# Heads in every fourth partition, x and the second context behind the first fills, and the last weights loaded later

## The chip, the cores and the metric

The kernel runs on one NeuronCore of a Trainium2 chip. The number that counts is the device time of one execution in microseconds. The kernel before was timed three times. One further execution was recorded by the profiler, and all rows below come from that one.

## What is computed

A cross-attention layer with an MLP behind it, for 8 batches of 256 queries over 1601 keys, width 256, 16 heads of 16.

```python
q = layer_norm(x) @ q_w + q_b ;  k = ctx @ k_w + k_b ;  v = ctx @ v_w + v_b      # per head of 16
attn = softmax(where(mask, q @ k.T / sqrt(16), min));  out = attn @ v
hidden = out @ cproj_w + cproj_b + x
y = gelu(layer_norm(hidden) @ fc_w + fc_b) @ proj_w + proj_b
return hidden + y
```

## The kernel before

Five instruction streams are written out by hand, one for each engine, and semaphores join them. For each batch K is computed with three products of split operands (a high and a low part), V and Q likewise. Four heads make a slot, so a batch has four slots. Each slot has 13 key tiles, hence 52 steps a batch, in 26 pairs. In a step TensorE multiplies the slot's `kst` (keys as weights) with `qst` (queries) into the PSUM tensor `S` (line 1119), ScalarE takes the exponential of all 1024 columns into `pr` (line 583), and TensorE multiplies `pr` with `vsl` into `O` (line 1126). Into the pairs of batch b are woven the projections of batch b+1 (`K_AT`, `V_AT`, pairs `XT_AT`, `Q_AT`) and the sampled maxima of a slot (`max_unit`, line 1106, pairs `MAX_AT`): slots 2 and 3 of the running batch at pairs 3 and 9, slots 0 and 1 of the next at pairs 15 and 21. Batch 0 has no batch ahead of it, so a head part does its projections and the maxima of its slots 0 and 1 first, with TensorE's order `v7, max(0,0), v8, max(0,1), v9, v10, max(1,0), v11, max(1,1), v12`.

K goes by way of HBM. VectorE splits it into `kpart` (lines 725, 728), SP stores it to `k_scr` (`store_k`, line 386), one unit for each of two halves of the width and four chunks of the keys, and `fill` brings it back into `kst`. A head of a slot takes 64 partitions of `kst`, two heads above each other (`g_` = 0, 1) and two side by side (`j`). Before, its first 32 partitions hold the high and low parts of K, 16 more the high part again, then comes the mask row (48) and the row of the maxima (49), and 14 partitions are unused. `qst` is laid out to match. One slot is 192 rows of 1601 floats of K, 96 rows of 512 floats of Q and four mask rows, 1.45 MB in all, in 10 DMAs, five for each half of the partitions. `kst` has places for four slots, which are used in turn.

DMAs are issued on two queues, SP's and ScalarE's (ACT's). Before the fills of batch 0 six small DMAs (`constant_rows`) write the rows of ones and the padding, on SP. On ACT the order of the head is: the high parts of the four context chunks (`high`), the loads of the second batch's context (`next_ctx`, four chunks, 1.64 MB), the second half of slot 0's fill, the fills of slots 1 and 2, and then the exponentials. `first_fill` for slot 2 waits until all eight K units of the batch have landed in HBM. On SP the load of the rest of x (12 row tiles, 1.57 MB, needed by VectorE at pair 6) stands behind the first batch's context. The mlp's weights `fc_raw` and `pj_raw` lie over the tiles of the projections; `load_mlp` on ACT waits for the last K, Q and V of batch 7, then issues two loads, and GpSimd splits the weights (lines 539 to 543). VectorE needs the first of the two low parts at pair 13 of batch 7, ACT both at step 36.

```python
for b in range(B):
    for n in range(STEPS):
        ...
        if n == 44 and b + 2 == B:
            load_mlp()
        ...
        exponential(first, b, n)
```

Of the kernel before, what the change touches and what calls it, by code (L numbers as in the profile page):

```python
# [42 lines left out]
H, HD = 16, 16  # L43
# [3 lines left out]
QT = LQ // P  # L47
# [16 lines left out]
MASKROW, MAXROW = 3 * HD, 3 * HD + 1  # L64
# [109 lines left out]
def build(nc, x, ctx_t, mask, w_kv, w_qc, fc, pj, cols, rows, ident, out):  # L174
    stack = ExitStack()
    with stack:
# [103 lines left out]
        o_zeroed, again_zeroed = sem("o_zeroed"), sem("again_zeroed")  # L280
# [62 lines left out]
        def fill(eng, s_, b, s, halves=range(2)):  # L343

            rows_of = k_scr[bass.ds(b, 1), s // 2].rearrange("o r (d h) t -> (o r d) h t", h=HM)
            for g_ in halves:
                r0, h0 = g_ * HALF, HG * (s % 2) + NJ * g_
                eng.dma_start(kst_d[r0:r0 + 2 * HD, s, :, 0:LK], rows_of[:, h0:h0 + NJ, 0:LK]).then_inc(s_.slot_in[s], 16)
                eng.dma_start(kst_d[r0 + 2 * HD:r0 + 3 * HD, s, :, 0:LK], rows_of[0:HD, h0:h0 + NJ, 0:LK]
                              ).then_inc(s_.slot_in[s], 16)  # L350
                eng.dma_start(kst_d[r0 + MASKROW:r0 + MASKROW + 1, s, :, 0:LK],
                              mask_scr[bass.ds(b, 1), :].unsqueeze(1).broadcast_to([1, NJ, LK])
                              ).then_inc(s_.slot_in[s], 16)
                for r, copies in ((0, 2), (1, 1)):
                    eng.dma_start(qst_d[r0 + 2 * HD * r:r0 + 2 * HD * r + copies * HD, s, :, :].rearrange("p j q -> p (j q)"),
                                  q_scr[bass.ds(b, 1), s // 2, r].rearrange("o (d h) q -> o d (h q)", h=HM)[
                                      :, :, h0 * LQ:(h0 + NJ) * LQ].broadcast_to([copies, HD, NJ * LQ])
                                  ).then_inc(s_.slot_in[s], 16)

        FILLS = 10  # L360
# [9 lines left out]
        def first_fill(eng, b, s, halves=range(2)):  # L370
# [8 lines left out]
            fill(eng, first, b, s, halves)  # L379

        @block.sync
        def _(sp):
# [38 lines left out]
            sp.dma_start(hid[:, 2 * QT:TOK, :], x[2 * QT:TOK].rearrange("n p d -> p n d")).then_inc(xrest_in, 16)  # L421
# [7 lines left out]
            sp.wait_ge(pads_set, 3)  # L429
            constant_rows()  # L430

            for c in range(CH):
                store_k(0, 0, c)
            store_q(0)
            first_fill(sp, 0, 0, [0])
# [3 lines left out]
            first_rows(0, 1)  # L439
# [916 lines left out]
```

## Time and profile before

| what | us |
|---|---|
| three runs | 768.25, 773.13, 775.28 |
| median | 773.13 |
| profiled execution, device time | 768.76 |
| its span, first to last instruction | 767.0 |
| TensorE busy in the span | 702.5 |
| ScalarE busy | 446.1 |
| VectorE busy | 371.3 |
| GpSimd busy | 120.9 |

Busy times are sums over instructions of an engine. The span is 1.8 us shorter than the device time of the same execution. Weight loads of TensorE run beside its products and are a row of their own (PEld).

### The profile page before, as it was taken

The numbers are of one execution on the slowest core, as the hardware profiler recorded it, in microseconds if no ns is written. First come the engines' busy times: TensorE is split into PE (matmuls) and PEld (weight loads), VectorE is DVE, ScalarE is ACT, GpSimd is POOL, SyncE is SP. The second block draws the span as 40 slices with busy tenths as digits, with TensorE's granted clock in tenths as the row PEclk, the third lists the DMA queues.
The fourth block names the chain that finished last, engine by engine and source line by source line (L and its number), as shares of the span: only waits on it lengthen the run. The fifth ranks groups of instructions, "written<-read, shape, count | busy, mean of one in ns | idle before, by whom it ended". The sixth has DMA issues, their size and how long they took to land.

```text
span 767.0 us, 16866 instructions
## 1 busy us (share of the span) xinstructions
PE 702.5 (92%) x7026; PEld 478.5 (62%) x7026; DVE 371.3 (48%) x824; ACT 446.1 (58%) x475; POOL 120.9 (16%) x90
## 2 busy tenths in 40 slices
PE   3657699899999999999999999999998978999997
PEld 3545466566656656666566566656664544597897
DVE  6643355265436534643464446534642331467663
ACT  3004366856676677567756775676566788733321
POOL 5222002200220032003201220131000600110010
PEclk9867799999999999999999999999999989999999
DMA  9787578657874788477938694878475800000000
GB/s 312 216 186 131 186 184 188 179 138 183 189 203 128 174 188 217 143 180 158 235 123 203 148 246 123 192 153 230 132 165 126 253 6 2 1 21 8 29 28 31
DMA packets 51275, 113.78 MB, mean 148 GB/s; under 512 B 7050, under 2 KB 40178, under 8 KB 49914
## 3 DMA queue, kind: packets, MB, share of 16 engines
q1 hardware_dynamic: 40700, 80.47, 44.5%
q10 hardware_dynamic: 10494, 32.17, 13.8%
q8 instruction: 58, 0.95, 0.6%
q14 instruction: 23, 0.19, 0.1%
HBM read 65.30 MB, written 47.06 MB: 146 GB/s over the span
## 4 chain that ended last, share of the span: by engine, by line
PE 76%; ACT 13%; DMA 5%; DVE 3%; issue 2%; ACTq 1%; DVEq 0%
PE O L1126 21%; PE S L1119 16%; ACT pr L583 11%; PE O L1056 10%; PE XB L1056 10%; PE O L1213 6%; PE S L1056 6%; DMA k_scr<-kpart 2%; DMA qst<-q_scr 2%; PE XB L1093 2%; PE XB L1153 2%; PE MB L1106 2%; DVE kpart L725 1%; DVE kpart L728 1%; DMA cols_s<-in_cols 1%
## 5 line engine op out<-in xcount | busy, mean ns | idle before, releaser
L583 ACT ACTIVATE pr<-S 128x1024 f32<-128x1024 f32 x416 | 400.6, 1024 | 188.6 <-PE S L1119 184.4
L1126 PE MATMUL O<-pr,vsl 128*17 128x256 f32 x3328 | 227.4, 388 | 1.3 <-DVE ot L790 1.3
L1119 PEld LDWEIGHTS S<-qst,kst 50*128 50x128 f32 x1664 | 117.1, 188 | 120.4 <-ACT pr L583 81.4
L1119 PE MATMUL S<-qst,kst 50*128 50x256 f32 x1664 | 171.7, 315 | 18.7 <-ACT pr L583 15.0
L1126 PEld LDWEIGHTS O<-pr,vsl 128*17 128x17 f32 x3328 | 75.3, 97 | 79.2 <-issue 17.7
L725 DVE TENSOR_SCALAR kpart<-O,cols_s 128x384 fp32r<-128x384 f32 x64 | 40.6, 635 | 120.7 <-PE O L1056 120.7
L771 DVE TENSOR_REDUCE mx<-MB 128x2 fp32r<-128x512 f32 x64 | 44.1, 690 | 79.0 <-PE MB L1106 79.0
L510 POOL CAST c_hi<-cT 128x768 fp32r<-128x768 f32 (+1 forms) x28 | 23.9, 852 | 348.0 <-DMA cT<-in_ctx_t 235.8
L1056 PE MATMUL XB<-w_hi,c_hi 128*128 128x256 f32 (+1 forms) x208 | 68.3, 328 | 2.1 <-DVE vsl L739 1.3
L739 DVE TENSOR_TENSOR vsl<-XB,rows_s 128x256 f32<-128x256 f32 (+1 forms) x104 | 43.3, 417 | 55.1 <-PE XB L1056 55.1
L1056 PE MATMUL O<-c_hi,w_hi 128*128 128x384 f32 (+1 forms) x128 | 52.6, 411 | 17.7 <-POOL c_lo L515 10.3
L515 POOL TENSOR_TENSOR c_lo<-cT,c_hi 128x768 fp32r<-128x768 f32 (+1 forms) x32 | 60.9, 1904 | 8.9 <-ACT c_hi L571 6.7
L1056 PE MATMUL XB<-w_lo,c_hi 128*128 128x256 f32 (+1 forms) x208 | 60.5, 291 | 0.0
L1056 PE MATMUL XB<-w_hi,c_lo 128*128 128x256 f32 (+1 forms) x208 | 60.1, 289 | 0.0
L601 ACT ACTIVATE g<-S,cols_s 128x512 f32<-128x512 f32 x32 | 22.1, 690 | 57.1 <-PE S L1056 52.8
L790 DVE STREAM_TRANSPOSE ot<-O 128x256 f32<-128x256 f32 x32 | 14.4, 450 | 78.0 <-PE O L1126 77.2
L1056 PEld LDWEIGHTS XB<-w_hi,c_hi 128*128 128x128 f32 (+1 forms) x208 | 40.1, 193 | 17.3 <-issue 9.0
L1056 PE MATMUL O<-c_lo,w_hi 128*128 128x384 f32 (+1 forms) x128 | 45.7, 357 | 0.0
L1056 PE MATMUL O<-c_hi,w_lo 128*128 128x384 f32 (+1 forms) x128 | 45.5, 355 | 0.0
L1106 PE MATMUL MB<-kst,qst 49*128 49x256 f32 x128 | 29.8, 314 | 16.3 <-DMA qst<-q_scr 16.2
L774 DVE TENSOR_REDUCE mx<-O 128x2 fp32r<-128x512 f32 x64 | 43.6, 682 | 0.0
L728 DVE SCALAR_TENSOR_TENSOR kpart<-O,cols_s,kpart 128x384 fp32r<-128x384 f32 x64 | 40.6, 635 | 2.3
(100 smaller groups left out, 825.6 us busy)
## 6 DMA issues: line engine op xcount, KB each, us to landing
kst<-k_scr SPq DMA_DIRECT2D x59, 400.2 KB
k_scr<-kpart SPq DMA_DIRECT2D x48, 384.0 KB, 8.0
v_scr<-vsl ACTq DMA_DIRECT2D x8, 1768.0 KB, 11.9
kst<-k_scr SPq DMA_DIRECT2D x59, 200.1 KB
cT<-in_ctx_t ACTq DMA_DIRECT2D x21, 384.0 KB, 7.6
k_scr<-kpart SPq DMA_DIRECT2D x16, 449.0 KB, 7.1
q_scr<-qpart SPq DMA_DIRECT2D x16, 256.0 KB, 2.5
qst<-q_scr SPq DMA_DIRECT2D x59, 64.0 KB
```

Source lines behind the costliest of these rows:

```text
L515: nc.gpsimd.tensor_tensor(c_lo[:, c, :, 0:n], cT[:, c, :, 0:n], c_hi[:, c, :, 0:n].bitcast(F32), ALU.subtract).then_inc(lo_done, 1)
L583: nc.scalar.activation(pr[:, n % PBUF, :], S[:, 2 * (n % 2):2 * (n % 2) + 2, :] .rearrange("p a n -> p (a n)"), ACT.Exp).then_inc(s_.exp_d ...
L725: nc.vector.tensor_scalar(kpart[:, i, 0, 0:n], KB[:, 0:n], bk_s[:, mt:mt + 1], None, ALU.add).then_inc(kh_done, 1)
L728: nc.vector.scalar_tensor_tensor(out=kpart[:, i, 1, 0:n], in0=KB[:, 0:n], scalar=bk_s[:, mt:mt + 1], in1=kpart[:, i, 0, 0:n].bitcast(F32), ...
L739: nc.vector.tensor_tensor(vsl[0:m, b % 2, :, kt, :].rearrange("p s (h w) -> p s h w", w=VW)[:, :, :, 0:HD], XB[0:m, 0:D].rearrange("p (s h ...
L771: nc.vector.tensor_reduce(mx[:, s % 2, :, j], MB[:, :].rearrange("p (q k) -> p q k", q=QT), AX.X, ALU.max, negate=True).then_inc(mb_taken, 1)
L774: nc.vector.tensor_reduce(mx[:, s % 2, :, NJ + j], KB.rearrange("p (q k) -> p q k", q=QT), AX.X, ALU.max, negate=True).then_inc(kb_taken, 1)
L1056: last = nc.tensor.matmul(dst, a, c, start=i == 0, stop=i == len(terms) - 1)
L1106: last = nc.tensor.matmul(bank[:, q * SAMPLE:(q + 1) * SAMPLE], query_set(rows_, s, j, q), kst[rows_, s, j, q * SAMPLE:(q + 1) * SAMPLE], ...
L1119: last = nc.tensor.matmul(S[:, 2 * (n % 2) + g_, j * LQ:(j + 1) * LQ], kst[rows_, s, j, kt * P:(kt + 1) * P], qst[rows_, s, j, :], start=T ...
L1126: last = nc.tensor.matmul(O[32 * h:32 * h + VW, 0, 0:LQ], vsl[:, par, s, kt, h * VW:(h + 1) * VW], pr[:, n % PBUF, h * LQ:(h + 1) * LQ], s ...
L1213: last = nc.tensor.matmul(O[:, n % 2, 0:D], w[:, i, cut], v[:, i, :], start=i == 0 and m == 0, stop=i == NI - 1 and m == 2)
```

## The change

K and Q rows of a head now lie at every fourth partition: partition 4d + part of each 64 holds width d, with part 0 the high, part 1 the low and part 2 the high part of K again. Part 3 holds the mask row at partition 3 and the maxima's row at 63; its other partitions are zero. One DMA of the fill now writes one part for both halves of the partitions, 32 partitions at a step of four, so a fill is 7 DMAs (`fill_k` three, `fill_q` three, `fill_mask` one) with the same bytes. Products with `kst` take 64 rows, not 50, those of the maxima 63, not 49. The host orders the columns of the K and Q weights by blocks of two heads, so that two rows of a DMA are neighbours in HBM.

The unused partitions must be zero once. GpSimd clears all of `qst` in place of the pads of `kst`, ACT copies these zeros over `kst` in eight instructions of 128x1664, and `constant_rows` waits for that and is moved behind the K stores of the first half. Slot 0's fill is split by part, not by partitions: parts 0 and 1 on SP, the rest on ACT. On ACT the second context's four loads are no longer ahead of the fills: one comes behind slot 0, one behind slot 1, two behind slot 2. On SP the rest of x is loaded behind the rows of maxima of slots 0 and 1, ahead of slot 3's fill. `load_mlp` moves from step 44 of batch 6 to step 4 of batch 7. What is changed behind `failed` is only run when a check of the result's scale fails.

```diff
--- before.py
+++ after.py
@@ -61,7 +61,8 @@
 CHUNK = [c for c in range(CH) for _ in range(NT[c])]
 HALF = P // 2
 NJ = HG // 2
-MASKROW, MAXROW = 3 * HD, 3 * HD + 1
+PARTS = HALF // HD
+MASKROW, MAXROW = PARTS - 1, HALF - 1
 KROWS = MAXROW + 1
 SCALE = 1.0 / float(np.sqrt(HD))
 EPS = 1e-5
@@ -277,7 +278,7 @@
         ln_steps, ln_root = sem("ln_steps"), sem("ln_root")
         good_steps, good_ready, flag_done = map(sem, ("good_steps", "good_ready", "flag_done"))
         xn_done, xb_done, xagain_done = map(sem, ("xn_done", "xb_done", "xagain_done"))
-        o_zeroed, again_zeroed = sem("o_zeroed"), sem("again_zeroed")
+        o_zeroed, again_zeroed, kst_zeroed = sem("o_zeroed"), sem("again_zeroed"), sem("kst_zeroed")
         mlpw_hi, mlpw_lo = sem("mlpw_hi"), sem("mlpw_lo")
 
         kb_ready, kb_taken, mb_ready, mb_taken, xb_ready, xb_taken = map(
@@ -340,24 +341,34 @@
             eng.dma_start(cT[:, c, :, 0:NK[c]], ctx_t[b, :, :, T0[c] * P:T0[c] * P + NK[c]].rearrange("k p t -> p k t")
                           ).then_inc(ctx_in[c], 16)
 
-        def fill(eng, s_, b, s, halves=range(2)):
-
-            rows_of = k_scr[bass.ds(b, 1), s // 2].rearrange("o r (d h) t -> (o r d) h t", h=HM)
-            for g_ in halves:
-                r0, h0 = g_ * HALF, HG * (s % 2) + NJ * g_
-                eng.dma_start(kst_d[r0:r0 + 2 * HD, s, :, 0:LK], rows_of[:, h0:h0 + NJ, 0:LK]).then_inc(s_.slot_in[s], 16)
-                eng.dma_start(kst_d[r0 + 2 * HD:r0 + 3 * HD, s, :, 0:LK], rows_of[0:HD, h0:h0 + NJ, 0:LK]
+        def fill_k(eng, s_, b, s, parts):
+
+            rows_ = slice(HALF * (s % 2), HALF * (s % 2 + 1))
+            for part in parts:
+                eng.dma_start(kst_d[part::PARTS, s, :, 0:LK],
+                              k_scr[bass.ds(b, 1), s // 2, part % 2, rows_, 0:LK].rearrange("o (p j) t -> (o p) j t", j=NJ)
                               ).then_inc(s_.slot_in[s], 16)
-                eng.dma_start(kst_d[r0 + MASKROW:r0 + MASKROW + 1, s, :, 0:LK],
-                              mask_scr[bass.ds(b, 1), :].unsqueeze(1).broadcast_to([1, NJ, LK])
+
+        def fill_q(eng, s_, b, s):
+
+            rows_ = slice(HALF * (s % 2), HALF * (s % 2 + 1))
+            for part, r in enumerate((0, 0, 1)):
+                eng.dma_start(qst_d[part::PARTS, s, :, :].rearrange("p j q -> p (j q)"),
+                              q_scr[bass.ds(b, 1), s // 2, r, rows_, :].rearrange("o (p j) q -> (o p) (j q)", j=NJ)
                               ).then_inc(s_.slot_in[s], 16)
-                for r, copies in ((0, 2), (1, 1)):
-                    eng.dma_start(qst_d[r0 + 2 * HD * r:r0 + 2 * HD * r + copies * HD, s, :, :].rearrange("p j q -> p (j q)"),
-                                  q_scr[bass.ds(b, 1), s // 2, r].rearrange("o (d h) q -> o d (h q)", h=HM)[
-                                      :, :, h0 * LQ:(h0 + NJ) * LQ].broadcast_to([copies, HD, NJ * LQ])
-                                  ).then_inc(s_.slot_in[s], 16)
-
-        FILLS = 10
+
+        def fill_mask(eng, s_, b, s):
+
+            eng.dma_start(kst_d[MASKROW::HALF, s, :, 0:LK],
+                          mask_scr[bass.ds(b, 1), :].unsqueeze(1).broadcast_to([2, NJ, LK])).then_inc(s_.slot_in[s], 16)
+
+        def fill(eng, s_, b, s):
+
+            fill_k(eng, s_, b, s, range(PARTS - 1))
+            fill_q(eng, s_, b, s)
+            fill_mask(eng, s_, b, s)
+
+        FILLS = 7
         ROWS_IN = 16 * HG
 
         def k_landed(eng, units):
@@ -367,7 +378,7 @@
 
         UK = 2 * CH
 
-        def first_fill(eng, b, s, halves=range(2)):
+        def fill_ready(eng, b, s):
 
             eng.wait_ge(q_out, 32 * (b + 1))
             k_landed(eng, UK * b + CH * (s // 2 + 1))
@@ -376,7 +387,11 @@
                 eng.wait_ge(ones_in, 16 * 6)
             else:
                 eng.wait_ge(first.scores_done, STEPS * (b - 1) + KT * (s + 1))
-            fill(eng, first, b, s, halves)
+
+        def first_fill(eng, b, s):
+
+            fill_ready(eng, b, s)
+            fill(eng, first, b, s)
 
         @block.sync
         def _(sp):
@@ -418,7 +433,6 @@
             load_ctx(sp, 0, 2)
             sp.dma_start(w_qc_s[:], w_qc).then_inc(wqc_in, 16)
             load_ctx(sp, 0, 3)
-            sp.dma_start(hid[:, 2 * QT:TOK, :], x[2 * QT:TOK].rearrange("n p d -> p n d")).then_inc(xrest_in, 16)
 
             sp.wait_ge(mask_steps, 4)
             sp.dma_start(some_scr.rearrange("o b -> b o"), some_b[:, 1:2]).then_inc(some_out, 16)
@@ -426,17 +440,19 @@
             sp.wait_ge(some_out, 16)
             sp.dma_start(some[:], some_scr[0].partition_broadcast(P)).then_inc(some_in, 16)
 
-            sp.wait_ge(pads_set, 3)
-            constant_rows()
-
             for c in range(CH):
                 store_k(0, 0, c)
+            sp.wait_ge(pads_set, 3)
+            sp.wait_ge(kst_zeroed, SLOTS * NJ)
+            constant_rows()
             store_q(0)
-            first_fill(sp, 0, 0, [0])
+            fill_ready(sp, 0, 0)
+            fill_k(sp, first, 0, 0, [0, 1])
             for c in range(CH):
                 store_k(0, 1, c)
             first_rows(0, 0)
             first_rows(0, 1)
+            sp.dma_start(hid[:, 2 * QT:TOK, :], x[2 * QT:TOK].rearrange("n p d -> p n d")).then_inc(xrest_in, 16)
             for b in range(B):
                 first_fill(sp, b, 3)
                 if b + 1 < B:
@@ -470,7 +486,7 @@
             with failed(sp):
                 for s in range(SLOTS):
                     sp.sem_inc(whole.mrow_in[s], ONE)
-                sp.wait_ge(pads_set, 11)
+                sp.wait_ge(pads_set, 12)
                 constant_rows()
                 sp.wait_ge(ones_in, 16 * 12)
                 sp.dma_start(hid[:], x.rearrange("n p d -> p n d")).then_inc(xagain_in, 16)
@@ -491,7 +507,7 @@
             nc.gpsimd.memset(ones[:], 1.0).then_inc(pads_set, 1)
             pool.wait_ge(pads_set, 1)
             nc.gpsimd.memset(ones[0:1, :], -MASKED).then_inc(pads_set, 1)
-            nc.gpsimd.memset(kst_d[:, :, :, LK:KP], 0.0).then_inc(pads_set, 1)
+            nc.gpsimd.memset(qst_d, 0.0).then_inc(pads_set, 1)
             nc.gpsimd.memset(cT[:, CH - 1, :, NK[-1]:NKM], 0.0).then_inc(pads_set, 1)
 
             def v_pads(par, before):
@@ -553,7 +569,10 @@
             y_low(first)
             with failed(pool):
                 pool.wait_ge(first.pj_ready, TOK)
-                nc.gpsimd.memset(kst_d[:, :, :, LK:KP], 0.0).then_inc(pads_set, 1)
+                for i in range(2):
+                    pool.wait_ge(first.out_done[i], 16 * TOK // 2)
+                nc.gpsimd.memset(kst_d, 0.0).then_inc(pads_set, 1)
+                nc.gpsimd.memset(qst_d, 0.0).then_inc(pads_set, 1)
                 pool.wait_ge(xagain_in, 16)
                 nc.gpsimd.tensor_tensor(hid[:], hid[:], bc_s.unsqueeze(1).broadcast_to([P, TOK, D]), ALU.add
                                         ).then_inc(xagain_done, 1)
@@ -631,11 +650,20 @@
             x_root(0, 2 * QT, XA_VAR)
             for c in range(2, CH):
                 high(c)
-            for c in range(CH):
+            zeros = qst_d.rearrange("p s j q -> p (s j q)")[:, 0:KP]
+            for s in range(SLOTS):
+                for j in range(NJ):
+                    nc.scalar.activation(kst[:, s, j, :], zeros, ACT.Copy).then_inc(kst_zeroed, 1)
+            fill_ready(act, 0, 0)
+            fill_k(act, first, 0, 0, [2])
+            fill_q(act, first, 0, 0)
+            fill_mask(act, first, 0, 0)
+            next_ctx(1, 0)
+            first_fill(act, 0, 1)
+            next_ctx(1, 1)
+            first_fill(act, 0, 2)
+            for c in range(2, CH):
                 next_ctx(1, c)
-            first_fill(act, 0, 0, [1])
-            first_fill(act, 0, 1)
-            first_fill(act, 0, 2)
             for b in range(B):
                 for n in range(STEPS):
                     if n == 10 and b == 0:
@@ -644,7 +672,7 @@
                         next_ctx(b + 2, CTX_AT.index(n))
                     if n == 48 and b + 1 < B:
                         store_v(b + 1)
-                    if n == 44 and b + 2 == B:
+                    if n == 4 and b + 1 == B:
                         load_mlp()
                     if b == 0 and n == 40:
                         x_root(2 * QT, TOK, XB_VAR)
@@ -1102,7 +1130,7 @@
                 bank_free(kb_taken, kb)
                 for q in range(QT):
                     for g_, (bank, ready) in enumerate(((MB[:, :], mb_ready), (KB, kb_ready))):
-                        rows_ = slice(g_ * HALF, g_ * HALF + MASKROW + 1)
+                        rows_ = slice(g_ * HALF, g_ * HALF + MAXROW)
                         last = nc.tensor.matmul(bank[:, q * SAMPLE:(q + 1) * SAMPLE], query_set(rows_, s, j, q),
                                                 kst[rows_, s, j, q * SAMPLE:(q + 1) * SAMPLE], start=True, stop=True)
                         if q == QT - 1:
@@ -1284,7 +1312,7 @@
                 pe.wait_ge(whole.slot_in[s], 16 * (FILLS + 1) * (b + 1))
                 for h in range(HG):
                     g_, j = h // NJ, h % NJ
-                    rows_ = slice(g_ * HALF, g_ * HALF + MASKROW + 1)
+                    rows_ = slice(g_ * HALF, g_ * HALF + MAXROW)
                     for i, (q, k, w) in enumerate(ALLKEYS):
                         pe.wait_ge(max_taken, ONE + USES * n + h * len(ALLKEYS) + i)
                         nc.tensor.matmul(MB[:, 0:w], query_set(rows_, s, j, q), kst[rows_, s, j, k:k + w],
@@ -1325,7 +1353,7 @@
         return a.reshape(-1, P, a.shape[-1]).transpose(1, 0, 2)
 
     def by_width(a):
-        return a.reshape(*a.shape[:-1], 2, HM, HD).swapaxes(-1, -2).reshape(a.shape)
+        return a.reshape(*a.shape[:-1], H // NJ, NJ, HD).swapaxes(-1, -2).reshape(a.shape)
 
     def by_slot(a):
         return a.reshape(SLOTS // 2, 2, HG, HD, a.shape[-1]).swapaxes(1, 2).reshape(a.shape)
```

## Rows read from the trace of the kernel before

**Rows 1.** Windows: length, busy PE, PEld, DVE, ACT, POOL; PEclk, DMA share, GB/s.

```profile
8.00:20.00 12.00, 7.51 (x36) 6.90 (x36) 10.45 (x28) 4.17 (x6) 7.54 (x4) 1.00 1.07 376
34.00:53.00 19.00, 11.43 (x54) 9.79 (x53) 7.19 (x14) 0.00 (x0) 3.50 (x3) 0.68 0.96 217
54.00:61.00 7.00, 2.23 (x10) 1.67 (x11) 1.10 (x4) 0.00 (x0) 0.83 (x1) 0.50 0.12 44
64.00:80.00 16.00, 10.48 (x94) 7.51 (x93) 5.62 (x12) 8.94 (x9) 4.34 (x3) 0.93 1.02 153
169.00:243.00 74.00, 73.06 (x802) 47.41 (x802) 35.65 (x78) 49.87 (x53) 12.31 (x9) 1.00 0.71 178
```

**Rows 2.** Timeline of TensorE in the head (start, length, what; idle before).

```profile
49.61 0.58 PE L1106 MATMUL MB<-kst,qst 49*128 49x256 f32 x1 [5.38 <-DMA qst<-q_scr]
...
60.70 0.58 PE L1106 MATMUL MB<-kst,qst 49*128 49x256 f32 x1 [4.16 <-DMA qst<-q_scr]
...
65.24 0.81 PE L1119 MATMUL S<-qst,kst 50*128 50x256 f32 x8
...
82.88 0.58 PE L1106 MATMUL MB<-kst,qst 49*128 49x256 f32 x1 [6.68 <-DMA qst<-q_scr]
...
83.60 1.91 PE L1126 MATMUL O<-pr,vsl 128*17 128x256 f32 x16
...
89.52 1.06 PE L1126 MATMUL O<-pr,vsl 128*17 128x256 f32 x16
```

**Rows 3.** The chain that ended last, in order of time, in the head.

```profile
42.84 18.23 DMA k_scr<-kpart
...
66.17 16.66 DMA qst<-q_scr
```

**Rows 4.** Timeline of ACT in the head.

```profile
14.66 0.94 ACT L571 ACTIVATE c_hi<-cT 128x900 fp32r<-128x900 f32 x1
...
61.31 0.32 ACTq L348 DMA_DIRECT2D kst<-k_scr  x1
...
66.93 1.28 ACT L583 ACT_TABLE_LOAD   x1 [51.33 <-issue]
68.22 3.77 ACT L583 ACTIVATE pr<-S 128x1024 f32<-128x1024 f32 x4
```

**Rows 5.** Timeline of SP's queue in the head.

```profile
18.95 0.80 SPq L407 DMA_DIRECT2D kst<-ones  x1
...
22.93 0.64 SPq L411 DMA_DIRECT2D qst<-ones  x1
...
31.19 0.89 SPq L392 DMA_DIRECT2D q_scr<-qpart  x2
34.11 0.35 SPq L348 DMA_DIRECT2D kst<-k_scr  x1
```

**Rows 6.** Timeline of GpSimd at the start.

```profile
1.36 0.51 POOL L494 MEMSET kst<- 128x504 f32 x1
```

**Rows 7.** Costliest groups on the page: weight loads of 50 and of 128 rows.

```profile
L1119 PEld LDWEIGHTS S<-qst,kst 50*128 50x128 f32 x1664 | 117.1, 188 | 120.4 <-ACT pr L583 81.4
...
L1056 PEld LDWEIGHTS XB<-w_hi,c_hi 128*128 128x128 f32 (+1 forms) x208 | 40.1, 193 | 17.3 <-issue 9.0
```

**Rows 8.** Timeline of ACT where batches 4 and 5 end.

```profile
443.93 6.87 ACT L583 ACTIVATE pr<-S 128x1024 f32<-128x1024 f32 x7
...
518.22 6.87 ACT L583 ACTIVATE pr<-S 128x1024 f32<-128x1024 f32 x7
```

**Rows 9.** Timeline of ACT where batch 6 ends.

```profile
591.89 2.86 ACT L583 ACTIVATE pr<-S 128x1024 f32<-128x1024 f32 x3 [3.14 <-issue]
...
597.23 11.85 ACT L583 ACTIVATE pr<-S 128x1024 f32<-128x1024 f32 x12 [1.57 <-PE S L1119]
```

**Rows 10.** Timeline of GpSimd: the mlp's weights.

```profile
601.51 1.89 POOL L539 CAST fc_hi<-fc_raw 128x2048 fp32r<-128x2048 f32 x1 [69.80 <-DMA pj_raw<-in_pj]
...
609.83 4.57 POOL L543 TENSOR_TENSOR pj_lo<-pj_raw,pj_hi 128x2048 fp32r<-128x2048 f32 x1
```

## The prediction

> **What bounds the kernel now.** I read the windows first, then the timeline of TensorE, then the chain that ended last. In a middle batch TensorE is busy for 73.1 of 74 us [rows 1]: nothing else can be gained there without taking work from it. In the head it is not. TensorE stands still before the sampled maxima of slots 0, 1 and 2 of batch 0, for 5.4, 4.2 and 6.7 us, each time until a slot's fill has landed [rows 2]. The chain names the transfers behind this: 18.2 us for the last store of K, then 16.7 us for slot 2's fill [rows 3].
>
> Why are these transfers slow? While context, weights and x are loaded, the 16 DMA engines are fully taken and move 376 GB/s. While slots 2 and 3 are filled and little else moves, they are as fully taken and move 153 GB/s; in a mixture of fills, K stores and leftovers it is 217. From 54 to 61 us the share is 0.12, which is 2 engines of 16, at 44 GB/s, and everybody waits for these two [rows 1]. One operation of the fill fits: the copy of Q's high part reads through a leading dimension of two copies. The mask row and the row of ones go to few partitions too, but are small.
>
> **Fills, the bytes.** A fill is 3x64 rows of 6404 B of K, 96 rows of 2048 B of Q and four mask rows: 1.45 MB, before and after. What changes is where they land. Before, the first K transfer of a half covers 32 neighbouring partitions, the second only 16. After, each covers 32 partitions spread over all 128, and Q has no leading dimension of two. The rate of such a transfer is in no row. Its bounds are the 153 GB/s of the fills and the 376 of loads into all partitions [rows 1]. I take 290, nearer to the loads, since the destination has the spread of the loads.
>
> The Trainium skill, page "SBUF — State Buffer", section on the DMA port swizzle, says that 0 to 63 reach only 8 of 16 ports, and gives 196 GB/s for 64 partitions against 328 for 128 at 1 MiB. The trace agrees in direction (153 against 376 GB/s [rows 1]). As an estimate by this page's ratio, the fills would go at 153x328/196 = 256 GB/s, and slot 1 would be 1.3 us later than in my sum. The Trainium skill, page "DMA: Bandwidth & Descriptors", section on why a DMA increments by 16, says that a DMA runs on the largest number of engines up to 16 that divides both slowest dimensions; for two copies that is 2, which the share of 0.12 bears out [rows 1].
>
> **Zeros and constants.** Eight copies of 128x1664 on ACT are new. 900 columns take 0.94 us [rows 4]. At the ratio of columns one takes 1.7 us; part of the 0.94 is fixed, so I take 1.55, and 12.4 for eight. They begin when the last high part is done, 15.6, and end at 28.0. ACT then did nothing until the fills, so they cost nothing by themselves. But the six constant DMAs wait for them. They took from 18.95 to 23.57, 4.6 us, on SP [rows 5]; now 28.0 to 32.6. The stores of Q stand behind them: they went at 31.19 and now at 32.6, so the fills can start at 35.5 and not 34.11, 1.4 us late [rows 5]. GpSimd's memset of 2048 columns in place of 504 (0.51 us [rows 6]) takes about 2 us, and the first context chunk's low part waits for ACT's high part several us longer: nothing.
>
> **Slot 0.** SP issues parts 0 and 1, ACT the other five DMAs in 2.8 us (10 took 61.31 to 66.93, 0.56 each [rows 4]). With some K stores between, 1.45 MB and 0.8 MB at 320 to 376 GB/s are there by about 42. TensorE's work ahead of these maxima ends at 44.2 (49.61 less 5.38 [rows 2]). This wait is gone; were the fill as slow as before, what remains is to 49.6 plus 1.4.
>
> **Slot 1 and the last K store.** Of what is queued from 35.5 on, SP's ring has 0.82 MB of parts and 1.64 MB of K, ACT's up to slot 1's end about as much: 4.9 MB in all. Of these 2.9 MB are fills, 10.0 us at 290 GB/s, and 2.0 MB are K and context, 5.3 us at 376. Both end at about 51. Bounds: 13 us at 376 throughout, so 48.5, and 22.6 us at 217, so 58. Before it was 60.70 and 61.06 [rows 2, 3]. What goes is the tail on two engines, and the second context and the rest of x (3.2 MB), which shared the queues.
>
> **Slot 2 and the first exponential.** ACT waits for all K in HBM, so to 51, issues 7 DMAs (3.9 us) and two context loads (0.9), loads its table (1.3 [rows 4]) and starts at 57.1, before at 68.22 [rows 4]: 11.1 us earlier. TensorE has its first scores ready 4.5 us behind slot 1's landing (60.70 to 65.24 [rows 2]), at 55.5, so ACT's issuing stays the late one. TensorE came to slot 2's maxima at 76.2 (82.88 less 6.68 [rows 2]), 8 us behind the first exponential, and will at 65.1. Slot 2 was issued by 66.9 and there at 82.9, 16 us; now it is issued by 55, ahead of the loads on its own queue, and needs about 6 to 8 us. So this wait, too, is gone. At this place the gain is 82.88 less 65.1, or 17.8 us. Behind the stall TensorE ran at half of its clock: a group of 16 products took 1.91 us at 83.6 and 1.06 at 89.5 [rows 2]. The 5.9 us between hold 3.3 us of work at full clock, so 2.6 us more. Head: 20.4.
>
> **What moves behind.** The last two context chunks are issued at 55 and land by 62. GpSimd needs 2.4 us for 768 columns (cast and subtraction of 2048 are 6.4 [rows 10]); at 74.3/26, 2.9 us a pair, TensorE wants the third chunk at pair 4 (68) and the fourth at pair 6 (74). The rest of x goes out at about 58, ahead of slot 3, 3.0 MB together, there before 70; VectorE wants x at pair 6, TensorE slot 3 at pair 9 (83). All at nothing; if the queues ran at 153 GB/s, the third chunk would be late by up to 5 us.
>
> **More rows in the products.** A weight load of 50 rows takes 188 ns and one of 128 rows 193 [rows 7]. If all 5 ns were due to rows, 14 more would cost 1 ns, on 1664 loads that run beside products. Nothing; at worst 1.5 us. Faster fills in the middle batches gain nothing either, for TensorE does not wait there [rows 1].
>
> **The last weights.** Where batch 6 ends, ACT waits 3.1 us before step 44 for the last V [rows 9]. The period of a batch is 518.22 less 443.93, 74.3 us [rows 8]. In batch 5, seven exponentials (47 to 51, 0, 1) end at 525.1; a period later is 599.4. In batch 6 step 1 is the sixth of the row at 597.23 and ends at 603.2 [rows 8, 9]. So the wait, and the half clock it leads to, costs 3.8 us. After, nothing is waited for at step 4, near 602. GpSimd began on the weights 10 us after ACT's wait was over, had the first low part 8.3 us later and all 12.9 us later [rows 9, 10]: now at 620 and 625. With step 1 ended at 599.4 and 0.98 us at least for each exponential, VectorE's pair 13 (step 26) is not before 624 and ACT's step 36 not before 633. Gain 3.8; its bounds are 2 (the weights a little late) and 4.
>
> **Sum.** 20.4 and 3.8 are 24.2 us. The profiled execution, 768.8, becomes 744.6. The median of the runs lies 4.4 above it, so the median becomes 773.1 less 24.2, 749. One per cent, 7.7 us, is about what a measurement of this kernel can tell from no change.
>
> **Rivals.** *The layout does nothing for the rate* (0.18). The engines are taken fully while they fill [rows 1], which can mean that each is slow at its rows whatever the partition. The Trainium skill, page "DMA: Bandwidth & Descriptors", section on issuing engines, says that all queues share the same 16 engines, which fits this as well. Then slot 1 and K land at 58, the first exponential is at 64, slot 2 is issued by 62 and, at 153 GB/s with the loads beside it, lands at about 74: 9 us gained there, 2 in the clock, 3.8 at the end: 15, so 758. *No transfer binds in the head* (0.15): at 376 GB/s slot 1 is there at 48.5, and 2.5 us more are gained: 746. *A new wait* (0.09): the constants, or chunk three of the context, take back 5 to 9 us: 756. *Spread rows are slower* (0.03): in a middle batch the DMA engines are taken for 0.71x74 = 53 us [rows 1]; four fills, 5.8 MB, are 38 of it at 153 GB/s, the rest 15. Once the fills take more than 59 us, so below 98 GB/s, DMA bounds every batch. At 85 GB/s a batch needs 83 us, 9 more in each of seven: 63 us lost against 10 gained, 826. *The head's gain is swallowed behind it* (0.05), by a transfer of batch 1 that I do not see: 769.
>
> **How the numbers follow.** My forecast, 749, has 0.50. Its bounds with rivals one to three give 741 to 760; what is left out is under 2 in 10. Faster by over 1% 0.92, within 1% 0.05, slower 0.03.
>
> **What would show it.** Right: no share of 0.12 in the head; no wait of TensorE for `qst` over 3 us; first exponential near 57; ACT without a wait before step 44 of batch 6; windows with only fills above 250 GB/s. Wrong: a window of fills at 150 GB/s, constants still in flight when the stores of Q have landed, GpSimd late with chunk three, or the middle batches at other than 74.3 us.

## The result and the profile after

| | before | after |
|---|---|---|
| median of four runs each, us | 770.69 (767.01 to 775.28) | 748.58 (746.95 to 749.94) |
| ratio, 95% interval | | 0.9709 (0.9646 to 0.9773) |
| profiled execution, device time | 768.76 | 748.42 |
| its span | 767.0 | 746.6 |

Faster by 2.9%. A fourth run of before has brought its median from 773.13 to 770.69. The forecast was 749. The profiled execution fell by 20.3 us, where the prediction's sum has 24.2. So the total was met with some luck, and where it came from is the matter of this text.

Windows of after, the same stretches as [rows 1] and three more in the head (length, busy PE, PEld, DVE, ACT, POOL; PEclk, DMA share, GB/s):

```profile
8.00:20.00 12.00, 8.22 (x29) 7.72 (x30) 9.50 (x27) 8.57 (x10) 7.54 (x4) 1.00 0.56 207
24.00:34.00 10.00, 6.77 (x26) 5.65 (x27) 5.25 (x11) 3.45 (x3) 0.12 (x1) 0.83 0.34 66
36.00:40.00 4.00, 3.25 (x21) 2.95 (x20) 1.58 (x4) 0.00 (x0) 0.00 (x0) 1.00 0.47 168
44.00:52.00 8.00, 5.13 (x26) 4.12 (x26) 3.68 (x8) 0.00 (x0) 2.25 (x2) 0.79 1.05 406
54.00:61.00 7.00, 6.53 (x31) 5.30 (x32) 3.55 (x7) 0.11 (x1) 2.66 (x2) 0.50 0.62 199
64.00:80.00 16.00, 15.96 (x168) 10.50 (x165) 10.84 (x19) 10.32 (x12) 6.96 (x5) 1.00 1.00 376
169.00:243.00 74.00, 73.06 (x804) 47.48 (x802) 35.76 (x79) 50.17 (x52) 12.30 (x9) 1.00 0.52 180
213.00:218.00 5.00, 5.00 (x61) 3.23 (x60) 3.73 (x11) 2.39 (x3) 0.00 (x0) 1.00 0.93 328
```

Read share and GB/s together. In a middle batch as many bytes move (180 against 178 GB/s) in less DMA time (0.52 against 0.71), and TensorE is busy for the same 73.06 us: cheaper transfers there are worth nothing. The last window is a slot's fill and the start of one store of K: 328 GB/s at 0.93. In the head the fall to 0.12 has gone. But from 24 to 34 us the DMA engines are two thirds idle, and from 36 to 40, when the first fill has been released, they still stand half idle.

Timeline of TensorE in the head of after (start, length, what, idle before), as in [rows 2]:

```profile
45.88 0.39 PE L1134 MATMUL MB<-kst,qst 63*128 63x256 f32 x1 [3.06 <-DMA kst<-mask_scr]
...
54.47 0.58 PE L1134 MATMUL MB<-kst,qst 63*128 63x256 f32 x1 [2.63 <-DMA kst<-mask_scr]
...
59.00 1.22 PE L1147 MATMUL S<-qst,kst 64*128 64x256 f32 x8
...
70.02 0.36 PE L1134 MATMUL MB<-kst,qst 63*128 63x256 f32 x1
```

The three waits of 5.4, 4.2 and 6.7 us [rows 2] are now 3.1, 2.6 and none. A second profiled execution of the same kernel (after_again, below) divides them otherwise, with no less in all:

```profile
47.01 0.58 PE L1134 MATMUL MB<-kst,qst 63*128 63x256 f32 x1 [5.93 <-DMA kst<-mask_scr]
...
54.41 0.58 PE L1134 MATMUL MB<-kst,qst 63*128 63x256 f32 x1 [0.47 <-DMA kst<-mask_scr]
```

The mask is named because it is the last piece of a fill to land; masks_early below tests whether it is slow. Slot 2's maxima, the row to compare, come at 70.02 and not 82.88, and TensorE is at full clock there.

Timeline of ACT in the head of after, as in [rows 4] (ACTq is its DMA issuing):

```profile
15.51 11.94 ACT L656 ACTIVATE kst<-qst 128x1664 fp32r<-128x1664 f32 x8
36.76 0.66 ACTq L348 DMA_DIRECT2D kst<-k_scr  x1
...
40.75 3.22 ACTq L348 DMA_DIRECT2D kst<-k_scr  x3
...
45.94 0.57 ACTq L362 DMA_DIRECT2D kst<-mask_scr  x1
...
55.20 1.88 ACTq L348 DMA_DIRECT2D kst<-k_scr  x3
...
60.89 1.28 ACT L602 ACT_TABLE_LOAD   x1 [33.45 <-issue]
62.19 3.95 ACT L602 ACTIVATE pr<-S 128x1024 f32<-128x1024 f32 x4
```

The chain that ended last has three long links in the head of after, in order of time:

```profile
15.60 11.86 ACT kst L656 x8
32.72 4.02 DMA q_scr<-qpart
45.94 8.49 DMA kst<-mask_scr
```

Zeros, then the store of Q, then slot 1's fill, which is now 8.5 us from its last issue to its landing; before, the last K store took 18.2 and slot 2's fill 16.7 [rows 3]. The prediction had the zeros cost nothing by themselves and 1.4 us through the constants. They are on the chain, but VectorE was done with Q's low part only at 31.62, and SP issued the store of Q at 32.23: without the zeros it could have gone 0.6 us earlier.

At the end, ACT of after goes into the last batch without the wait of 3.14 us of [rows 9], and the weights are issued behind step 4:

```profile
576.64 1.02 ACT L602 ACTIVATE pr<-S 128x1024 f32<-128x1024 f32 x1 [0.97 <-PE S L1147]
...
577.56 8.02 ACT L602 ACTIVATE pr<-S 128x1024 f32<-128x1024 f32 x8
585.24 0.35 ACTq L641 DMA_DIRECT2D fc_raw<-in_fc  x1
```

GpSimd began on them at 595.78 and had the last low part at 608.8; nothing waited for it.

**Where the 20 us are.** The product for Q of the next batch comes once in a batch, in pair 5, and tells how far the whole pipeline has been shifted. In batch 4, counted from 0, it started at 391.80 before and at 376.81 after; the third line is from weights_only (below), whose head is the code of before:

```profile
391.80 1.99 PE L1093 MATMUL XB<-attT,w_qc_s 128*128 128x256 f32 x8
...
376.81 1.99 PE L1121 MATMUL XB<-attT,w_qc_s 128*128 128x256 f32 x8
...
389.38 1.99 PE L1093 MATMUL XB<-attT,w_qc_s 128*128 128x256 f32 x8
```

So between these two executions the head gave 15.0 us. One execution is no exact measure of it: weights_only is 2.4 us ahead of before with the same head, and after_again, the same kernel as after, is at 378.64, 1.8 behind it.

In the last batch the row of exponentials below is 18.7 us earlier, before and after in this order. That is 3.7 more, and it came where ACT no longer waits for the weights.

```profile
611.26 3.77 ACT L583 ACTIVATE pr<-S 128x1024 f32<-128x1024 f32 x4 [2.18 <-PE S L1119]
...
592.57 3.77 ACT L602 ACTIVATE pr<-S 128x1024 f32<-128x1024 f32 x4 [2.11 <-PE S L1147]
```

Another 1.4 us came in that batch behind ACT's table loads. The granted clock of TensorE was 0.83 from 620 to 640 us before and 0.91 from 600 to 620 after, so it ran at half clock for 6.8 us and for 3.6.

### The profile page after: what moved, and what is told of

It is laid out like the page before. It is cut to its first block, busy times and chain, and to the rows that moved or that the text cites. A ratio compares the mean times of both kernels' runs of the same rounds, so it can differ in the third digit from the quotient of the medians.

```text
span 746.6 us, 16779 instructions
## 1 busy us (share of the span) xinstructions
PE 698.5 (94%) x7026; PEld 476.5 (64%) x7026; DVE 375.6 (50%) x824; ACT 458.0 (61%) x483; POOL 122.6 (16%) x90
## 4 chain that ended last, share of the span: by engine, by line
PE 77%; ACT 15%; DMA 2%; DVE 2%; issue 1%; ACTq 1%; SPq 1%; DVEq 0%
PE O L1154 22%; PE S L1147 16%; ACT pr L602 12%; PE XB L1084 11%; PE O L1084 10%; PE O L1241 6%; PE S L1084 6%; PE XB L1181 2%; PE XB L1121 2%; PE MB L1134 2%; ACT kst L656 2%; DMA kst<-mask_scr 1%; DMA cols_s<-in_cols 1%; DMA q_scr<-qpart 1%; ACTq L348 1%
## 5 line engine op out<-in xcount | busy, mean ns | idle before, releaser
L1154 PE MATMUL O<-pr,vsl 128*17 128x256 f32 x3328 | 224.8, 385 | 1.3 <-DVE ot L818 1.3
L1147 PEld LDWEIGHTS S<-qst,kst 64*128 64x128 f32 x1664 | 116.0, 186 | 115.7 <-ACT pr L602 77.5
L1147 PE MATMUL S<-qst,kst 64*128 64x256 f32 x1664 | 170.7, 313 | 14.9 <-ACT pr L602 11.0
L1154 PEld LDWEIGHTS O<-pr,vsl 128*17 128x17 f32 x3328 | 74.9, 97 | 78.1 <-issue 15.7
L620 ACT ACTIVATE g<-S,cols_s 128x512 f32<-128x512 f32 x32 | 22.1, 689 | 57.2 <-PE S L1084 52.8
L1084 PEld LDWEIGHTS O<-c_hi,w_hi 128*128 128x128 f32 x128 | 24.9, 195 | 24.7 <-issue 13.1
```

The source lines that it names most:

```text
L1084: last = nc.tensor.matmul(dst, a, c, start=i == 0, stop=i == len(terms) - 1)
L1147: last = nc.tensor.matmul(S[:, 2 * (n % 2) + g_, j * LQ:(j + 1) * LQ], kst[rows_, s, j, kt * P:(kt + 1) * P], qst[rows_, s, j, :], start=T ...
L1154: last = nc.tensor.matmul(O[32 * h:32 * h + VW, 0, 0:LQ], vsl[:, par, s, kt, h * VW:(h + 1) * VW], pr[:, n % PBUF, h * LQ:(h + 1) * LQ], s ...
```

## The experiments

Kernels of one chip share their runs of before, whose medians were 768.3 (13 runs), 768.5 (7) and 768.1 (11) on chips A, B and C. "At pair 5" is the start of the product above, in the one profiled execution of each kernel; before it is 391.80. Equal heads differ there by up to 2.4 us, so smaller differences in this column say nothing.

| kernel | chip | median | ratio (95%) | at pair 5 |
|---|---|---|---|---|
| layout_only | A | 752.0 | 0.9767 (0.9748, 0.9787) | 377.14 |
| order_only | A | 769.9 | 1.0028 (0.9999, 1.0057) | 388.75 |
| weights_only | A | 764.1 | 0.9932 (0.9911, 0.9953) | 389.38 |
| q_split | A | 757.7 | 0.9854 (0.9810, 0.9898) | 381.96 |
| slot2_on_sp | B | 745.6 | 0.9703 (0.9681, 0.9724) | 373.99 |
| zeros_shared | B | 750.7 | 0.9773 (0.9742, 0.9805) | 379.14 |
| masks_early | B | 750.0 | 0.9759 (0.9732, 0.9785) | 377.89 |
| all_three | B | 749.7 | 0.9756 (0.9727, 0.9785) | 375.77 |
| after_again | C | 749.4 | 0.9744 (0.9713, 0.9775) | 378.64 |
| layout_and_weights | C | 749.8 | 0.9769 (0.9740, 0.9797) | 376.36 |
| split_and_weights | C | 754.8 | 0.9822 (0.9792, 0.9852) | 381.97 |
| loads_in_gap | C | 743.8 | 0.9684 (0.9659, 0.9709) | 371.14 |

**layout_only**: after, with the loads' order and the weights' place of before.

```
+            for c in range(CH):
+                next_ctx(1, c)          # ahead of the zeros
...                                      # and the rest of x behind load_ctx(sp, 0, 3)
-                    if n == 4 and b + 1 == B:
+                    if n == 44 and b + 2 == B:
```

> The new layout of kst and qst with its fills, zeros and constants, but the second context and the rest of x ahead of the fills and the last weights where the kernel before has them. Theory (layout and order each give a part): fills no longer move at 153 GB/s and no tail on two engines is left, so that slot 2's wait of 6.7 us goes; but the zeros now start behind the four context loads, at 19, so the fills start near 39. Span 7 to 11 us below before, DMA share of a middle batch 0.52 as after. Rival (the layout does nothing for the rate, the order gave it all): within 3 us of before or slower by the late zeros, share near 0.71.

It alone gives 16 us, more than the 7 to 11 expected. ACT's queue shows what the old order costs here: the loads hold the zeros back from 15.5 to 19.2, so the fills start at 41.04 and not 36.76.

```profile
16.72 2.44 ACTq L341 DMA_DIRECT2D cT<-in_ctx_t  x2
19.21 11.97 ACT L658 ACTIVATE kst<-qst 128x1664 fp32r<-128x1664 f32 x8 [3.58 <-POOL c_lo L531]
41.04 0.68 ACTq L348 DMA_DIRECT2D kst<-k_scr  x1
```

The fills start 4.3 us later, and yet at pair 5 the kernel is level with after: less stood in the queues, and one wait of TensorE is left, for slot 0; slots 1 and 2 are not waited for.

```profile
50.48 0.58 PE L1132 MATMUL MB<-kst,qst 63*128 63x256 f32 x1 [6.05 <-DMA kst<-mask_scr]
```

**order_only**: before, with the second context and the rest of x behind the fills.

```
-            for c in range(CH):
-                next_ctx(1, c)
             first_fill(act, 0, 0, [1])
+            next_ctx(1, 0)
             first_fill(act, 0, 1)
+            next_ctx(1, 1)
             first_fill(act, 0, 2)
+            for c in range(2, CH):
+                next_ctx(1, c)
```

> The kernel before with only the loads of the second context and of the rest of x moved behind the fills. Theory: these 3.2 MB shared the queues until about 45 us, so slots 0 and 1 come 5 to 6 us earlier, but the fills still go at 153 GB/s and still end in a tail on two engines: slot 2's wait stays at several us. Span 5 to 9 us below before. Rival (order gives it all): 15 to 17 us below before.

No gain, where 5 to 9 us were expected. Timeline of TensorE of order_only: the waits have moved, not gone.

```profile
44.89 0.58 PE L1108 MATMUL MB<-kst,qst 49*128 49x256 f32 x1 [3.99 <-DMA qst<-q_scr]
...
58.61 0.58 PE L1108 MATMUL MB<-kst,qst 49*128 49x256 f32 x1 [6.78 <-DMA qst<-q_scr]
...
75.14 0.39 PE L1108 MATMUL MB<-kst,qst 49*128 49x256 f32 x1 [1.09 <-DMA qst<-q_scr]
...
80.65 0.44 PE L1058 MATMUL O<-c_hi,w_hi 128*128 128x384 f32 x1 [3.33 <-POOL c_lo L515]
```

The last row is new: GpSimd waited 15.7 us for the third context chunk, now at the end of a slow queue. It is the price that the prediction gave for queues at 153 GB/s (up to 5 us), and in the old layout it is paid. In this trace the kernel is 5.6 us ahead of before at pair 5 of batch 0 (85.79 against 91.43) and 0.7 at its end. Part of the loss can be seen: 1.6 us of TensorE at 100.4, where VectorE had waited 3.5 us for a store of K, and a granted clock of 0.80 in the 26 us around the wait for the weights, where before has 0.93.

**weights_only**: before, with the one line of `load_mlp` moved.

> The kernel before with only the load of the mlp's weights moved to step 4 of batch 7. Theory: ACT's 3.1 us of waiting before step 44 of batch 6 is gone and 3.8 us with it. Rival (ACT or TensorE waits elsewhere in batch 7 instead, or GpSimd is late): less than 1.5 us.

0.68% of 768 is 5.2 us (3.6 to 6.8), the medians lie 4.1 apart, and the prediction had 3.8. Its trace has the two parts that after has: counted from pair 5 of batch 4, it gains 3.8 us up to ACT's table loads in the last batch and 1.2 behind them, where the half clock is again 3.6 us long and not 6.8. On top of the layout the weights can't be told from nothing: layout_only lies 16.3 us below its before and layout_and_weights 18.3 below its own, on another chip, but their ratios are 0.9767 and 0.9769.

**q_split**: before, with the one DMA of Q's high part into two copies made two DMAs.

```
-                for r, copies in ((0, 2), (1, 1)):
...
-                                      :, :, h0 * LQ:(h0 + NJ) * LQ].broadcast_to([copies, HD, NJ * LQ])
+                for i, r in enumerate((0, 0, 1)):
...
+                                      0, :, h0 * LQ:(h0 + NJ) * LQ]
...
-        FILLS = 10
+        FILLS = 12
```

> The kernel before with the two copies of Q's high part written by two DMAs of 16 partitions instead of one that reads through a leading dimension of two: 12 DMAs a fill in place of 10, same bytes, same partitions. Theory: the tail at a share of 0.12 between 54 and 61 us is this transfer on two engines; it goes, slot 1 lands 5 to 6 us earlier, and slot 2 2 to 3, so the span falls by 4 to 7 us although ACT issues two more DMAs for each slot (1.1 us each). Rival (the tail is the mask rows, or something else on two engines): the tail stays and the span is the same or 1 to 3 us longer.

This small edit is worth 11 us, nearly two thirds of what the layout gives, where 4 to 7 were expected. TensorE's waits for the three fills, 16.2 us before, are 4.2 in all. Windows of q_split:

```profile
54.00:61.00 7.00, 4.72 (x23) 3.75 (x22) 2.96 (x6) 0.00 (x0) 0.00 (x0) 0.50 0.60 177
64.00:80.00 16.00, 14.33 (x143) 9.97 (x142) 7.18 (x14) 11.04 (x12) 2.11 (x2) 0.91 1.04 200
169.00:243.00 74.00, 73.05 (x802) 47.19 (x800) 35.81 (x78) 50.15 (x52) 12.30 (x9) 1.00 0.76 179
```

Where 0.12 stood there is 0.60: the two-engine tail was this operation. The rate of full engines rose with it, from 153 to 200 GB/s, but stayed low (200 at 1.04, where after has 376 at 1.00), and the middle batch takes even more DMA time, 0.76. So the pattern of the copy and the rate of a fill are two causes, and the layout mends both. The Trainium skill, page "DMA: Bandwidth & Descriptors", section on why a DMA increments by 16, has the rule by which a leading dimension of two gets two engines; removing it removed the 0.12, which bears it out.

**slot2_on_sp**: after, with slot 2's fill issued by SP behind the first rows of maxima, and the last two context chunks behind that. ACT loads its table at 47.6 and waits for scores.

```
             first_rows(0, 0)
+            first_fill(sp, 0, 2)
             first_rows(0, 1)
+            for c in range(2, CH): ... load_ctx(sp, 1, c)
-            first_fill(act, 0, 2)
```

> The changed kernel with slot 2's fill issued by SP, between the rows of maxima of slots 0 and 1, and the last two context loads behind those of slot 1, so that ACT has nothing to wait for or issue between slot 1's fill and its exponentials. Theory: the first exponential waited for 7+2 issues behind K's landing (55.2 to 62.2) while the scores were ready at 60.2; it now starts at 60.3 or, since the table is loaded earlier, at the scores; gain 1.5 to 2.5 us. Rival (TensorE at half clock sets the start, or slot 2's rows and the third context chunk come later from SP and stop TensorE): no gain, or 1 to 3 us slower.

The first exponential is at 58.91 and not 62.19, and the kernel is 3 to 4 us faster than after: 745.6 against 748.6 and 749.4, measured on other chips. 1.5 to 2.5 were expected. Timeline of ACT of slot2_on_sp:

```profile
47.64 1.28 ACT L606 ACT_TABLE_LOAD   x1 [20.13 <-DMA k_scr<-kpart]
58.91 1.94 ACT L606 ACTIVATE pr<-S 128x1024 f32<-128x1024 f32 x2 [9.99 <-PE S L1148]
```

**zeros_shared**: after, with half of the zeros as four memsets on GpSimd.

```
+            for s in range(SLOTS):
+                nc.gpsimd.memset(kst_d[:, s, 1, :], 0.0).then_inc(kst_zeroed, 1)
-                for j in range(NJ):
-                    nc.scalar.activation(kst[:, s, j, :], zeros, ACT.Copy).then_inc(kst_zeroed, 1)
+                nc.scalar.activation(kst[:, s, 0, :], zeros, ACT.Copy).then_inc(kst_zeroed, 1)
```

> The changed kernel with half of the zeros written by GpSimd (four memsets of 1664 columns behind its low parts of the context) and half by ACT. Theory: the zeros end near 25 instead of 27.5, the constants on SP at 29.7, and then the stores of Q wait for VectorE's low part at 31.6: the fills start 0.6 us earlier at most, so the span moves by less than 1 us. Rival (the zeros hold the whole head): the fills start 2.5 us earlier and the span falls by 2 to 3 us.

The zeros were all written at 24.3 and not 27.5, but the fills went out later, at 40.12. GpSimd's row, and the rows of VectorE beside it:

```profile
18.59 5.75 POOL L545 MEMSET kst<- 128x1664 f32 x4
```

```profile
18.90 5.47 DVE L726 TENSOR_SCALAR rs<-rs 128x4 f32<-128x4 f32 x1
24.41 0.16 DVE L728 TENSOR_TENSOR rs<-rs 128x4 f32<-128x4 f32 x1
```

VectorE's work for Q stands behind this, and the store of Q was issued at 37.18, not 32.23. So this run doesn't show what fewer zeros would give by themselves.

**masks_early**: after, with the mask rows of slots 0 to 2 sent first.

```
+            act.wait_ge(kst_zeroed, SLOTS * NJ)
+            act.wait_ge(mask_out, 16)
+            for s in range(3):
+                fill_mask(act, first, 0, s)
             fill_ready(act, 0, 0)
```

> The changed kernel with the mask rows of slots 0 to 2 written by ACT behind the zeros, 8 us before the fills, and not as the last DMA of each fill. Theory: slot 0's maxima waited for the mask's DMA, issued at 39.4 and landed at 45.8, on two engines behind the K parts; without it slot 0 lands up to 2 us earlier and ACT's issuing is 0.6 us shorter for each slot, so slot 1 and K too: 1.5 to 3 us gained. Rival (all bytes of the slot land then, the mask is only the last to report): no wait shrinks by more than 0.6 us, gain under 1 us.

TensorE goes on with slots 0 and 1 at 45.02 and 53.47, 0.9 and 1.0 us earlier than in after and now with `qst` named as last, and the median shows no gain. The mask was mostly what reported last.

**all_three**: the three edits before this together, to see whether they add. They don't.

> The changed kernel with slot 2 on SP, shared zeros and early masks together. Theory: gains add up to 3 to 6 us below the changed kernel. Rival: they stand behind each other (the transfer of 5.3 MB sets slot 1 and all of K), and 1 to 2 us are left.

The memsets' cost comes along: fills at 39.52, first exponential at 61.45, and all of slot 2's gain on SP is spent.

**after_again, layout_and_weights, split_and_weights**, six runs each on one chip: after itself; after with the order of before; and q_split with the late weights.

> The changed kernel itself, to stand beside the next three on the same chip: 0.970 to 0.974 of before. The earlier interval, 0.965 to 0.977, was too wide to compare variants with.

> The changed kernel with the second context and the rest of x back ahead of the fills: layout and late weights, without the new order. Theory (formed on the runs before: the order alone gained nothing, layout 18 us and the weights 5 add up to all of the gain): within 2 us of the changed kernel. My theory from the prediction (3.2 MB ahead of the fills cost the head some us): 3 to 5 us slower.

> The kernel before with two edits only: the two copies of Q's high part by two DMAs, and the late weights. No new layout, no zeros, no new order. Theory (the two edits are independent): 0.9854 x 0.9932 = 0.979 of before, 752 us; 5 to 6 us slower than the changed kernel, which is what the fills' higher rate in the new layout is worth. Rival (with the tail gone the rate hardly matters): within 2 us of the changed kernel.

After against layout_and_weights is what the order is worth: 749.4 against 749.8, and by the ratios 0.25%, 1.9 us, with intervals that overlap. No gain can be shown, and 3 to 5 us are not excluded by the ends of the intervals. After against split_and_weights is what the rest of the change, the spread partitions above all, is worth above the repaired copy: 5.4 us.

**loads_in_gap**: slot2_on_sp, with the second context loaded before and behind the zeros, and the rest of x behind the first four K stores, where DMA stood idle.

```
+            for c in range(2):
+                next_ctx(1, c)          # ahead of the zeros
             zeros = ...
+            for c in range(2, CH):
+                next_ctx(1, c)          # behind them
             fill_ready(act, 0, 0)
```

> The changed kernel with slot 2 filled from SP, and the second context and the rest of x loaded between 14 and 34 us, when the DMA engines have nothing to do in the changed kernel (share 0.3), half of them before ACT's zeros and half behind. Theory: slot 1 and the last K store lose 0.8 MB beside them, 1 to 2 us, and nothing is late behind: 742 to 745 us, the fastest. Rival (leftovers of these loads delay K's first stores and so the stores of Q): as slot2_on_sp or 1 to 2 us slower.

It is the fastest of all, 5.6 us below after on the same chip. But it holds slot2_on_sp as well, which by itself gave 3 to 4. Against that kernel it is 1.8 us faster, measured on another chip, with ratios of 0.9684 and 0.9703 whose intervals overlap, so the loads' own part is not shown. Its window and its first exponential:

```profile
24.00:34.00 10.00, 6.28 (x23) 5.44 (x24) 5.79 (x11) 3.13 (x3) 3.02 (x3) 0.79 0.83 236
```

```profile
57.63 1.94 ACT L603 ACTIVATE pr<-S 128x1024 f32<-128x1024 f32 x2 [11.34 <-PE S L1147]
```

The loads go out largely in a stretch that after leaves at 0.34 (236 GB/s and not 66), the fills start no later (36.32), slot 1 is waited for no more, and slot 0 for 1.91 us.

## Why the prediction was right, and where it was not

**The mechanism** was right: DMA bound the head, for two reasons that the windows showed, two engines of 16 and 153 GB/s at full engines. q_split and split_and_weights separate them: 11 us for the copy, and 5.4 us for what the layout has above it. That a copy with a leading dimension of two stood behind 0.12 was an inference, and it held.

**The fills' rate**: taken 290, measured 328 with part of one store of K beside them and 406 for the mixture from 44 to 52 us. The first rival, that the layout does nothing for the rate, had 0.18 and is excluded by these windows; its price of 758 is near what split_and_weights, which leaves the rate as it was, measured (754.8). That spread rows are slower is excluded as well: a middle batch takes 0.52, less than the 0.71 of before. That no transfer binds in the head is excluded by the waits that are left, 3.1 and 2.6 us, and that the gain is swallowed behind the head by the 18.7 us in the last batch. No new wait came for the constants or for the third chunk of the context.

**Slot 0 and 1, the terms that were mis-sized.** "The fills can start at 35.5" was 36.76. The zeros and the six constants ended half a us before what was said (27.45 and 32.2), but from the issue of Q's store to the first fill it took 4.5 us where 2.9 was carried over. "This wait is gone" was wrong: slot 0 is waited for 3.1 us, and 5.9 in after_again, over the 3 us that the prediction named as its limit. "Both end at about 51" was 54.5 and 55.2. The bytes over the rate were right, and 406 GB/s is even more than was taken; what the sum lacked is the time in which the transfers are issued. A DMA over every fourth partition takes 0.63 us to issue (three of them 1.90), slot 1's last one went out at 45.94, and from 36 to 40 us the engines were at 0.47. The sum treated the 4.9 MB as queued from 35.5 on.

**Slot 2 and the first exponential**: 57.1 was 62.19. 4.2 of the 5.1 us are K landing late, 0.9 the issuing (5.7 us, not 4.8). slot2_on_sp shows that ACT's issuing was on the path, as the prediction had it. The gain at slot 2's maxima was 12.9 us where 17.8 was forecast; with the clock the head was 15.0 where 20.4 was forecast. A stretch at half clock in the projections is no part of this: after has one between 26 and 30 us, where eight products for Q took 3.49 us and not 1.97, before has one from about 31 us on, and after_again has none up to 36 us and is no earlier at pair 5 (378.64).

**The order of the loads** is the attribution that failed. "What goes is the tail on two engines, and the second context and the rest of x (3.2 MB)": the second half was given part of the gain. order_only gained nothing, and in the new layout no gain can be shown. In the old one, the displaced loads became the next wait. They were taken out of a stretch in which DMA has room (0.34 from 24 to 34 us in after) and put behind the fills, where it is at 1.05 and 1.00. loads_in_gap puts them back there without a loss; whether it gains by that is not shown.

**The last weights**: 3.8 was forecast, with a bound of 4. The traces of after and weights_only have 3.7 and 3.8 us for this wait, so the term was right. They have 1.4 and 1.2 more behind the table loads, which the sum doesn't hold; together that is the 5 us that weights_only measured. Whether the second part belongs to the late weights is not shown: the half clock there lasts 6.8 us in all four traces with the early weights, but also in three of the ten with the late ones (masks_early, all_three, loads_in_gap), and in zeros_shared there is none.

**Products with 64 rows** cost nothing, as said: the weight load is 186 ns where 188 stood [rows 7].

```profile
L1147 PEld LDWEIGHTS S<-qst,kst 64*128 64x128 f32 x1664 | 116.0, 186 | 115.7 <-ACT pr L602 77.5
```

**Why 749 was met all the same.** This part was luck. The span gained 20.4 us, not 24.2. But the sum was made against a median 4.4 us above the profiled execution, and with a fourth run that median fell by 2.4; in the later runs before stood at 768.1 to 768.5. By medians after gained 22.1 us in its own runs and 18.6 in after_again. A forecast made from the profiled execution's own time, 768.8 less 24.2, would have said 744.6, and been 3.8 too low.

What stays open: whether the order in the new layout is worth nothing or some us; whether the late weights shorten the half clock behind the table loads; and what in the layout raises the rate. A transfer now has spread partitions, but there are also fewer and more equal transfers, and their rows are neighbours in HBM. No run has these apart.

## What to carry to other kernels

Divide the DMA share of a stretch by one sixteenth: a share near 0.12 in a stretch where everybody waits is a transfer on two engines, and its access pattern's leading dimension is the place to look, before its bytes are. Read share and GB/s side by side: full engines at less than half of the load rate here went with transfers into blocks of neighbouring partitions, and moving other loads out of the way only moved the wait. And before a load is put behind something urgent, look for a stretch where the share is low: in loads_in_gap it cost nothing there. And add the issuing of an urgent batch of transfers to its time, not only its bytes.

## What the runs showed of the hardware

- A fill of 32 partitions at distance four ran at 328 GB/s. Fills of blocks of 32 and 16 neighbouring partitions ran at 153, and at 200 when the copy on two engines was made two DMAs (q_split). The Trainium skill, page "SBUF — State Buffer", section on the DMA port swizzle, gives 328 GB/s for 128 partitions and 196 for the first 64, both at 1 MiB, and says that what counts is how many of 16 ports the partitions reach; it has no rate for spread ones, but by its table every fourth partition reaches all 16. These rates agree with it in direction. That the partitions alone make the difference is not shown.
- Issuing had its own price: 0.63 us for a DMA over every fourth partition. Before, one transfer of K took 0.32 or 0.35 [rows 4, 5], and the mean of a fill's ten was 0.56 [rows 4]. In order_only, in a stretch at a share of 1.06, one DMA took 7 us to issue on SP, and the next went out behind it at 73.48; why is not shown:

```profile
66.37 7.06 SPq L348 DMA_DIRECT2D kst<-k_scr  x1
```

- VectorE's operation on four columns took 5.47 us beside four memsets of GpSimd (0.17 in after), and went on when they ended. It ended with them, and the path of Q's store runs through VectorE.
